# Evacuating and accumulating the expert products on VectorE instead of ScalarE and GpSimd, with another order of the steps in the queue

## The chip, the cores and the metric

The kernel runs on all 8 cores of one Trainium2 chip. Each core computes one of the eight sequences of the batch, with no exchange between them. The time is that of the slowest core, in device microseconds; lower is better. A core has TensorE (PE in the profile; its weight loads are PEld), VectorE (DVE), ScalarE (ACT), GpSimd (POOL) and SyncE (SP), each working through its own list of instructions in order.

## The reference, cut to what matters

```python
# x: (8, 4096, 1024); 16 heads of 64, chunks of 128
q, k = elu(x @ Wq.T + bq) + 1, elu(x @ Wk.T + bk) + 1
v = x @ Wv.T + bv
# per chunk of 128 tokens, state (S, z) carried on:
scores = tril(qi @ ki.T)
num = scores @ vi + qi @ S
den = sum(qi * (cumsum(ki) + z), -1)
out = num / den; S += ki.T @ vi; z += sum(ki)
x = layernorm(x + out @ Wo.T + bo)
# mixture: 8 experts, 1024 x 1024, all computed
gates = softmax(x @ gate_w.T + gate_b)
w = gates where among the two largest, else 0
ffn = sum_e w[:, e] * (x @ expert_w[e].T + expert_b[e])
x = layernorm(x + ffn)
```

## The kernel before

One sequence of 4096 tokens is cut into 8 superchunks (`s`) of 512 tokens, each of 4 chunks (`c`) of 128. The Python program writes one instruction list per engine; an engine takes its list strictly in that order, and `B.wait` puts a semaphore wait into it. So the order in which the program emits work is the order of each engine. A superchunk goes through these stages:

- **Projections** (`proj_core`, L371). Q and K are computed in two waves each of 32 matmuls of 512 columns (L384) into the PSUM buffers `q2`, `q3`; after each wave `emit_phi` evacuates four tiles (two ScalarE activations L407, L412 and one VectorE operation L418 each), and then `ffn_drain(..., limit=2)` (L396) emits up to two steps of the expert queue of the superchunk before. Behind K come the transposes of K (L438) with copies on VectorE (L447), and V (L460, L466) with ScalarE evacuation (L476). Then `ln2_out(s-1)` writes the output of the superchunk before.
- **Scan** (L1029 to L1046). For each chunk: scores (L565), the update of the state S (`sz_part`, L616, L623, L637), the numerator and denominator (`numden_div`, L681, L686), and, one chunk behind, `tail_chunk` (transpose L729, output projection L747 and L753, residual L767, first layer norm) and `tail_b` (cast, transpose L808, gates L825 to L868). Each of these steps hands over from TensorE to VectorE or ScalarE and back. Behind `tail_b(s, c-1)` stands `ffn_drain(s, limit=3)` (L1042).
- **Expert stretch** (L1052 to L1054). `x_stream(s+1)` is emitted first: 8 loads of `xT` pieces on POOL's queue into two landing buffers, each followed by a cast on VectorE (L366). Then `ffn_drain` takes all but `hold = 6` steps of the queue; those six are left for the next projections. In the last superchunk nothing is held.

The expert queue `ffnq` of a superchunk has 36 steps: 4 bias steps (`emit_ffn_bias`, 2 matmuls, L897) and then 32 expert steps (expert outer, chunk inner; `emit_ffn_exp`, 16 matmuls of 512 columns, L924). `ffn_drain` takes steps from the head only, and stops when the head's chunk has not gone through `tail_b` yet. Steps use the PSUM buffers `q0` and `q1` in turn; the scan uses `q0` and `q1` too. A step's product is evacuated by ScalarE into one of two `ffntmp` buffers (L910, L938, the latter with the gate as scale), and GpSimd adds it to `x1f` (`acc_pool`, L884).

The weights: 12 matrices a superchunk (Q, K, V, O, then experts e0 to e7, numbers `m` 0 to 11) pass through three SBUF slots. `free_and_feed(mat)` is called when a matrix has been used for the last time; it emits the load of the next matrix of the sequence into the freed slot, half on SP's queue and half on POOL's. Q and K (`m < 2`) are loaded in 8 pieces of 256 KB, even ones on SP's queue and odd ones on POOL's, each waiting for the piece before it on its queue (L286). In the first superchunk the weights come as f32 in halves through a landing buffer that takes the third slot, are cast by VectorE and ScalarE in turn (L261, L264) and are stored as bf16 for the superchunks behind it.

Of the kernel before, what the change touches and what calls it, by code (L numbers as in the profile page):

```python
# [88 lines left out]
def build():  # L89
# [39 lines left out]
    ffn_tmp = [sb(f"ffntmp{j}", [128, 1024], F32) for j in range(2)]  # L129
# [206 lines left out]
    ffn_tmp_i = [0]  # L336
    ffn_tmp_free = [[], []]
# [33 lines left out]
    def proj_core(s):  # L371
        def proj_qk(mat, dstbf, donearr, bias_col):
            src = wb[wslot[mat]]
            vpe_f = [None] * KB
            for wv in range(2):
# [20 lines left out]
                ffn_drain(s_cur[0], limit=2)  # L396
# [479 lines left out]
    def acc_pool(c, evac_ev):  # L876
        j2 = evac_ev[2]
        B.wait("POOL", evac_ev[0], evac_ev[1])
        if stt_val[c] is None:
            B.wait("POOL", "cdv", x1_apply[c])  # L880
        else:
            B.wait("POOL", "cpl", stt_val[c])
        B.wait("POOL", "dtap", tap_guard[0])
# [5 lines left out]
        return vadd  # L889

    def emit_ffn_bias(c, qi):
# [14 lines left out]
        j2 = ffn_tmp_i[0]  # L906
        ffn_tmp_i[0] ^= 1
        B.wait("ACT", "cpe", vpe)
        B.waits("ACT", ffn_tmp_free[j2])
        vac = B.op("ACT", lambda e, qi=qi, j2=j2: e.activation(  # L910
            ffn_tmp[j2][:], quad[qi][:], AF.Copy), inc="cac")
        qset(qi, (0, 1), [("cac", vac)])
        acc_pool(c, ("cac", vac, j2))
# [227 lines left out]
```

How the kernel before makes its waits and increments, by code:

```python
    def wait(self, eng, cname, val):  # L56
        if val is None or val <= 0:
            return
        w = self.waited[eng]
        if w.get(cname, 0) >= val:
            return
        w[cname] = val
        h = self.ctr[cname][0]
        self.streams[eng].append(lambda e, h=h, v=val: e.wait_ge(h, v))
# [14 lines left out]
        def run(e, fn=fn, h=h, k=k):  # L79
            fn(e).then_inc(h, k)
```

## Time and profile before

| | |
|---|---|
| Time, median of two runs | 2881.48 us (2866.7 and 2896.25) |
| Profiled execution, its own time | 2877.57 us |
| Its span, first to last instruction, slowest core (core 6) | 2875.8 us |
| Busy: PE, PEld | 1881.8 us (65%), 911.1 us (32%) |
| Busy: DVE, ACT, POOL | 700.0 us (24%), 858.0 us (30%), 816.5 us (28%) |
| Granted TensorE clock, mean of a core | 0.785 to 0.791 of full speed |
| Spans of the eight cores | 2850.6 to 2875.8 us |
| HBM | 105 GB/s over the span |

The largest shares of the chain of work that ended last:

```profile
PE 49%; DMA 15%; ACT 12%; DVE 11%; issue 10%; POOL 1%; DVEq 0%; ACTq 0%; SPq 0%; POOLq 0%
```

The profile is of one execution, on its slowest core. Busy time of PE includes overlap between matmuls. In the timeline a row has start, duration, engine, line, operation, output and inputs, count, and in brackets the idle time before it with what ended it; rows of one engine that follow each other closely are merged, and matmul records can be missing by a few in a row. The granted clock is a share of 2.4 GHz: 1.2 GHz would be 0.5.

### The profile page before, as it was taken

The numbers are of one execution on the slowest core, as the hardware profiler recorded it, in microseconds if no ns is written. First come the engines' busy times: TensorE is split into PE (matmuls) and PEld (weight loads), VectorE is DVE, ScalarE is ACT, GpSimd is POOL, SyncE is SP. The second block draws the span as 40 slices with busy tenths as digits, with TensorE's granted clock in tenths as the row PEclk, the third lists the DMA queues.
The fourth block names the chain that finished last, engine by engine and source line by source line (L and its number), as shares of the span: only waits on it lengthen the run. The fifth ranks groups of instructions, "written<-read, shape, count | busy, mean of one in ns | idle before, by whom it ended". The sixth has DMA issues, their size and how long they took to land.

```text
span 2875.8 us, 27448 instructions; the slowest of 8 cores (2850.6 to 2875.8 us)
## 1 busy us (share of the span) xinstructions
PE 1881.8 (65%) x9992; PEld 911.1 (32%) x10144; DVE 700.0 (24%) x1168; ACT 858.0 (30%) x974; POOL 816.5 (28%) x553
## 2 busy tenths in 40 slices
PE   1464455764799449864598547974499646994496
PEld 0132222332344224332244323432244323442243
DVE  1232300143202431043202332034211432024301
ACT  1322223322233223332234222332233222332232
POOL 1000234200462006410273005520174004620065
PEclk8665678875799559975699758995599757995698
DMA  5530366520333213430144103341144202432031
GB/s 176 199 140 15 121 232 231 164 86 15 110 125 123 76 44 131 126 132 14 60 147 147 74 15 125 120 150 37 52 140 135 106 15 103 132 117 81 37 107 69
DMA packets 63354, 303.99 MB, mean 106 GB/s; under 512 B 8172, under 2 KB 8428, under 8 KB 43766
## 3 DMA queue, kind: packets, MB, share of 16 engines
q1 hardware_dynamic: 34326, 163.80, 16.6%
q0 software_dynamic: 28896, 138.43, 14.0%
q8 instruction: 83, 1.36, 0.2%
q14 instruction: 49, 0.40, 0.0%
HBM read 260.26 MB, written 41.94 MB: 105 GB/s over the span
## 4 chain that ended last, share of the span: by engine, by line
PE 49%; DMA 15%; ACT 12%; DVE 11%; issue 10%; POOL 1%; DVEq 0%; ACTq 0%; SPq 0%; POOLq 0%
PE q L924 23%; PE q L747 6%; DMA wb<-escr 6%; DMA wb<-ewT 4%; PE q L460 4%; PE q L384 4%; DMA xtl<-xT 2%; PE q L753 2%; PE q L466 2%; PE q L565 2%; ACT L838 1%; DVE x1f L767 1%; DVE S_f L637 1%; ACT wb L264 1%; DMA out<-osb 1%
## 5 line engine op out<-in xcount | busy, mean ns | idle before, releaser
L884 POOL TENSOR_TENSOR x1f<-ffntmp,x1f 128x1024 f32<-128x1024 f32 x288 | 674.7, 2350 | 1330.1 <-ACT ffntmp L910 996.1
L924 PE MATMUL q<-wb,x1t_bf 128*128 128x512 bf16 x4015 | 914.8, 387 | 74.9 <-ACT ffntmp L938 63.0
L924 PEld LDWEIGHTS q<-wb,x1t_bf 128*128 128x128 bf16 x4096 | 406.4, 100 | 583.1 <-issue 121.8
L938 ACT ACTIVATE ffntmp<-q,w_all 128x1024 f32<-128x1024 f32 x256 | 285.5, 1117 | 552.6 <-PE q L924 483.9
L384 PE MATMUL q<-xt_bf,wb 128*128 128x512 bf16 x1001 | 241.8, 393 | 143.2 <-DMA wb<-escr 56.9
L747 PE MATMUL q<-wb,attnTb 128*128 128x512 bf16 x480 | 179.4, 554 | 54.8 <-ACT attnTb L738 54.8
L418 DVE SCALAR_TENSOR_TENSOR qt_bf<-etmp 128x512 bf16<-128x512 f32 x64 | 44.2, 693 | 630.6 <-ACT etmp L412 630.6
L198 POOL DMA_DIRECT2D wb<-escr x126 | 69.3, 550 | 442.3 <-PE q L466 213.3
L384 PEld LDWEIGHTS q<-xt_bf,wb 128*128 128x128 bf16 x1024 | 100.6, 100 | 279.1 <-issue 173.8
L565 PE MATMUL q<-qt_bf,ktz 128*128 128x128 bf16 x512 | 53.3, 287 | 141.2 <-DVE qtz L543 141.2
L460 PE MATMUL q<-wb,xt_bf 128*128 128x512 bf16 x496 | 123.7, 403 | 15.0 <-DVE ktm_bf L447 13.0
L808 PE MATMUL q<-id_bf,x1c_bf 128*128 128x128 bf16 x256 | 32.7, 307 | 150.3 <-ACT x1c_bf L801 150.3
L767 DVE TENSOR_TENSOR x1f<-q,x0c 128x1024 f32<-128x1024 f32 x32 | 39.2, 1225 | 323.9 <-PE q L753 323.9
L747 PEld LDWEIGHTS q<-wb,attnTb 128*128 128x128 bf16 x512 | 66.5, 134 | 160.2 <-issue 150.6
L781 ACT ACT_TABLE_LOAD x25 | 32.1, 1283 | 282.5 <-DVE mnv L778 282.5
L366 DVE CAST xt_bf<-xtl 128x512 bf16<-128x512 f32 x64 | 91.0, 1438 | 96.6 <-DMA xtl<-xT 96.4
L681 PE MATMUL q<-vext_bf,msc_bf 128*128 128x65 bf16 x512 | 42.5, 206 | 105.0 <-DVE msc_bf L585 92.0
L530 ACT ACTIVATE ktz<-kt_bf,pmask_s 128x1024 bf16<-128x1024 bf16 x64 | 69.9, 1140 | 90.0 <-PE q L565 83.8
L565 PEld LDWEIGHTS q<-qt_bf,ktz 128*128 128x128 bf16 x512 | 46.2, 132 | 149.9 <-issue 149.9
L418 DVE SCALAR_TENSOR_TENSOR kt_bf<-etmp 128x512 bf16<-128x512 f32 x64 | 44.3, 692 | 188.9 <-ACT etmp L412 188.8
L864 PE MATMUL q<-id_bf,w_bfs 128*8 128x128 bf16 x32 | 8.5, 264 | 122.2 <-DVE w_bfs L857 122.2
L407 ACT ACTIVATE etmp<-q,bqc_s 128x512 f32<-128x512 f32 x64 | 44.7, 699 | 144.3 <-PE q L384 135.8
(85 smaller groups left out, 1729.8 us busy)
## 6 DMA issues: line engine op xcount, KB each, us to landing
wb<-escr SPq DMA_DIRECT2D x70, 1024.0 KB, 5.1
wb<-escr POOLq DMA_DIRECT2D x70, 1024.0 KB, 6.2
wb<-ewT SPq DMA_DIRECT2D x16, 2048.0 KB
escr<-wb SPq DMA_DIRECT2D x12, 2048.0 KB, 7.8
xtl<-xT POOLq DMA_DIRECT2D x64, 256.0 KB, 3.3
x0c<-x POOLq DMA_DIRECT2D x32, 512.0 KB, 4.3
out<-osb POOLq DMA_DIRECT2D x32, 512.0 KB, 2.9
wb<-escr SPq DMA_DIRECT2D x56, 256.0 KB, 2.9
```

The costliest lines, as they stand in the source:

```text
L198: return B.op(eng, lambda e, o=out_ap, i=in_ap: e.dma_start(o, i), inc=cname, k=16)
L366: vc = B.op("DVE", lambda e, k=k, j=j: e.tensor_copy(xt_bf[:, k * 512:(k + 1) * 512], xt_land[j][:]), inc="cdv")
L384: fn = lambda e, src=src, k=k, f=f: e.matmul(quad[2 + (f % 4) // 2][:, ((f % 4) % 2) * 512:((f % 4) % 2 + 1) * 512], src[:, k * 1024 + f * ...
L418: e.scalar_tensor_tensor(d[:, f * 512:(f + 1) * 512], et[:], 1.0, et2[:], ALU.min, ALU.add), inc="cdv")
L460: B.op("PE", lambda e, src=src, k=k, c=c, qi=qi, hh=hh: e.matmul(quad[qi][:, hh * 512:(hh + 1) * 512], xt_bf[:, k * 512 + c * 128: k * 512 ...
L530: vkz = B.op("ACT", lambda e, c=c, par=par, mcol=mcol: e.activation(ktz[:].rearrange("p (h w) -> p h w", w=128)[:, par::2, :], kt_bf[:].re ...
L565: fn = lambda e, h=h, f=f, c=c, qi=qi, hh=hh: e.matmul(quad[qi][:, hh * 128:(hh + 1) * 128], ktz[:, h * 128:(h + 1) * 128], qt_bf[:, f * 5 ...
L747: B.op("PE", lambda e, src=src, k=k, hh=hh, j=j: e.matmul(quad[0][:, hh * 512:(hh + 1) * 512], attnT_bfp[j][:, k * 128:(k + 1) * 128], src ...
L767: vres = B.op("DVE", lambda e, j=j, c=c: e.tensor_tensor(x1f[:, c * 1024:(c + 1) * 1024], quad[0][:], x0c[j][:], ALU.add), inc="cdv")
L884: vadd = B.op("POOL", lambda e, c=c, j2=j2: e.tensor_tensor(x1f[:, c * 1024:(c + 1) * 1024], ffn_tmp[j2][:], x1f[:, c * 1024:(c + 1) * 102 ...
L924: fn = lambda e, src=src, k=k, c=c, qi=qi, hh=hh: e.matmul(quad[qi][:, hh * 512:(hh + 1) * 512], x1t_bf[:, c * 1024 + k * 128: c * 1024 + ...
L938: vac = B.op("ACT", lambda e, c=c, qi=qi, e_i=e_i, j2=j2: e.activation(ffn_tmp[j2][:], quad[qi][:], AF.Copy, scale=w_all[:, c * 8 + e_i: c ...
```

## The change

`ffntmp` and `acc_pool` go. A step's product is now taken from PSUM by one VectorE operation, `scalar_tensor_tensor`, that multiplies it by the gate (or by 1.0 in a bias step) and adds it to `x1f` in place; the buffer `q0` or `q1` is free when that is done. The waits that ScalarE and GpSimd had stand on VectorE's list. The queue is filled with the 32 expert steps first and the 4 bias steps behind them. `hold` is 12 instead of 6, and the limit after each projection wave is 3 instead of 2. One more `ffn_drain(s, limit=2)` stands behind `numden_div` in each chunk. A count per expert says when its weights are free; in this order it says so at the same step as before. `ln2_out` waits for VectorE's counter instead of GpSimd's.

```diff
@@ proj_qk
-                ffn_drain(s_cur[0], limit=2)
+                ffn_drain(s_cur[0], limit=3)
@@ acc_pool goes
-        vadd = B.op("POOL", lambda e, c=c, j2=j2: e.tensor_tensor(
-            x1f[:, c * 1024:(c + 1) * 1024], ffn_tmp[j2][:],
-            x1f[:, c * 1024:(c + 1) * 1024], ALU.add), inc="cpl")
-        stt_val[c] = vadd
-        ffn_tmp_free[j2] = [("cpl", vadd)]
+    def acc_wait_dve(c):
         if stt_val[c] is None:
-            B.wait("POOL", "cdv", x1_apply[c])
+            B.wait("DVE", "cdv", x1_apply[c])
         else:
-            B.wait("POOL", "cpl", stt_val[c])
+            B.wait("DVE", "cdv", stt_val[c])
@@ emit_ffn_exp (emit_ffn_bias likewise, with 1.0 for the gate)
-        B.wait("ACT", "cpe", vpe)
-        B.wait("ACT", "cdv", w_done[c])
-        B.waits("ACT", ffn_tmp_free[j2])
-        vac = B.op("ACT", lambda e, c=c, qi=qi, e_i=e_i, j2=j2: e.activation(
-            ffn_tmp[j2][:], quad[qi][:], AF.Copy,
-            scale=w_all[:, c * 8 + e_i: c * 8 + e_i + 1]), inc="cac")
-        qset(qi, (0, 1), [("cac", vac)])
-        vadd = acc_pool(c, ("cac", vac, j2))
+        B.wait("DVE", "cpe", vpe)
+        B.wait("DVE", "cdv", w_done[c])
+        acc_wait_dve(c)
+        B.wait("DVE", "dtap", tap_guard[0])
+        vstt = B.op("DVE", lambda e, c=c, qi=qi, e_i=e_i:
+                    e.scalar_tensor_tensor(
+                        x1f[:, c * 1024:(c + 1) * 1024],
+                        quad[qi][:],
+                        w_all[:, c * 8 + e_i: c * 8 + e_i + 1],
+                        x1f[:, c * 1024:(c + 1) * 1024],
+                        ALU.mult, ALU.add), inc="cdv")
+        stt_val[c] = vstt
+        qset(qi, (0, 1), [("cdv", vstt)])
@@ ffn_drain
+            pick = None
             step = ffnq[0]
             c = step[-1]
-            if c > ffn_done_c[0]:
+            if c <= ffn_done_c[0]:
+                pick = 0
+            if pick is None:
+                if limit is None:
+                    raise RuntimeError("ffn_drain: no ready step on full drain")
                 break
-            ffnq.pop(0)
+            step = ffnq.pop(pick)
...
-                if c == CPS - 1:
+                exp_cnt[e_i] += 1
+                if exp_cnt[e_i] == CPS:
                     free_and_feed(4 + e_i)
@@ the main loop
+            for e_i in range(NE):
+                exp_cnt[e_i] = 0
+                for cc in range(CPS):
+                    ffnq.append(("e", e_i, cc))
             for cc in range(CPS):
                 stt_val[cc] = None
                 ffnq.append(("b", cc))
-            for e_i in range(NE):
-                for cc in range(CPS):
-                    ffnq.append(("e", e_i, cc))
...
                 prev_attn_evs = numden_div(s, c)
+                if stage >= 4:
+                    ffn_drain(s, limit=2)
                 if c < CPS - 1:
                     scores_part(s, c + 1)
...
-            hold = 6 if s + 1 < nsc else 0
+            hold = 12 if s + 1 < nsc else 0
             ffn_drain(s, limit=max(0, len(ffnq) - hold))
```

## Rows read from the trace of the kernel before

**Rows 1.** Windows, superchunk 3: us; busy (count) of PE, PEld, DVE, ACT, POOL; clock; DMA.
```profile
1084.00:1170.00 86.00, 85.05 (x378) 38.14 (x386) 12.09 (x6) 26.63 (x24) 61.42 (x35) 0.97 0.40 141
1170.00:1235.00 65.00, 57.32 (x255) 25.21 (x258) 8.31 (x12) 24.62 (x35) 26.54 (x20) 0.97 0.41 123
...
1266.00:1418.00 152.00, 65.61 (x513) 38.56 (x516) 55.40 (x113) 41.06 (x50) 13.41 (x15) 0.59 0.16 59
```

**Rows 2.** Timeline, a bias step in the scan, and an output projection of superchunk 4.
```profile
988.46 0.26 PE L864 MATMUL q<-id_bf,w_bfs 128*8 128x128 bf16 x1 [3.81 <-DVE w_bfs L857]
989.26 1.01 PE L897 MATMUL q<-ebias,wT_all 8*128 8x512 bf16 x2 [0.53 <-DVE wT_all L868]
...
990.42 1.02 ACT L910 ACTIVATE ffntmp<-q 128x1024 f32<-128x1024 f32 x1 [3.71 <-PE q L897]
...
991.59 1.03 PE L616 MATMUL q<-vext_bf,ktm_bf 128*64 128x64 bf16 x16 [1.32 <-ACT ffntmp L910]
...
997.64 6.18 PE L747 MATMUL q<-wb,attnTb 128*128 128x512 bf16 x15 [1.64 <-ACT attnTb L738]
...
1295.78 5.59 PE L747 MATMUL q<-wb,attnTb 128*128 128x512 bf16 x15 [1.86 <-ACT attnTb L738]
```

**Rows 3.** Timeline, start of the expert stretch of superchunk 3, last two rows superchunk 4.
```profile
1083.12 0.74 DVE L366 CAST xt_bf<-xtl 128x512 bf16<-128x512 f32 x2
...
1084.28 4.02 PE L924 MATMUL q<-wb,x1t_bf 128*128 128x512 bf16 x9
...
1088.52 8.40 PE L924 MATMUL q<-wb,x1t_bf 128*128 128x512 bf16 x38 [0.22 <-issue]
...
1093.57 11.57 POOL L884 TENSOR_TENSOR x1f<-ffntmp,x1f 128x1024 f32<-128x1024 f32 x5
1095.48 10.39 DVE L366 CAST xt_bf<-xtl 128x512 bf16<-128x512 f32 x2 [3.02 <-DMA xtl<-xT]
...
1432.37 8.04 DVE L366 CAST xt_bf<-xtl 128x512 bf16<-128x512 f32 x2 [2.94 <-DMA xtl<-xT]
...
1434.24 4.85 PE L924 MATMUL q<-wb,x1t_bf 128*128 128x512 bf16 x11 [3.06 <-ACT ffntmp L938]
```

**Rows 4.** Timeline, end of that expert stretch and the projections behind it.
```profile
1170.11 1.11 ACT L938 ACTIVATE ffntmp<-q,w_all 128x1024 f32<-128x1024 f32 x1 [2.34 <-PE q L924]
1171.43 2.34 POOL L884 TENSOR_TENSOR x1f<-ffntmp,x1f 128x1024 f32<-128x1024 f32 x1 [1.11 <-ACT ffntmp L938]
...
1173.71 0.57 POOL L198 DMA_DIRECT2D wb<-escr  x1
...
1188.15 1.02 PE L384 MATMUL q<-xt_bf,wb 128*128 128x512 bf16 x4 [1.84 <-DMA wb<-escr]
...
1195.92 7.07 PE L384 MATMUL q<-xt_bf,wb 128*128 128x512 bf16 x31
...
1199.84 0.55 POOL L198 DMA_DIRECT2D wb<-escr  x1
...
1218.43 1.86 PE L384 MATMUL q<-xt_bf,wb 128*128 128x512 bf16 x4 [2.49 <-DMA wb<-escr]
...
1227.80 7.07 PE L384 MATMUL q<-xt_bf,wb 128*128 128x512 bf16 x31
```

**Rows 5.** Timeline, from the last K tile to V.
```profile
1240.60 4.61 DVE L447 CAST ktm_bf<-q 128x1024 bf16<-128x1024 f32 x4
...
1243.11 4.63 PE L460 MATMUL q<-wb,xt_bf 128*128 128x512 bf16 x15 [0.22 <-issue]
```

**Rows 6.** Lines of the whole span: the VectorE group nearest to the new operation.
```profile
L767 DVE TENSOR_TENSOR x1f<-q,x0c 128x1024 f32<-128x1024 f32 x32 | 39.2, 1225 | 323.9 <-PE q L753 323.9
```

**Rows 7.** Timeline, end of the program.
```profile
2852.51 1.11 ACT L938 ACTIVATE ffntmp<-q,w_all 128x1024 f32<-128x1024 f32 x1 [2.34 <-PE q L924]
...
2862.93 0.69 DVE L973 BATCH_NORM_STATS2 lnst<-x1f 128x6 f32<-128x512 f32 x1
```

**Rows 8.** Waits of the whole span, a row of the first superchunk's weight staging.
```profile
DVE wb L261 <- DMA wb<-ewT: 161.9, 6, 36.8
```

More of the change, by code:

```diff
@@ L128, in build @@
     x1f = sb("x1f", [128, 4096], F32)
-    ffn_tmp = [sb(f"ffntmp{j}", [128, 1024], F32) for j in range(2)]
     x1c_bf = sb("x1c_bf", [128, 1024], BF16)
@@ L335, in build @@
     stt_val = [None] * CPS
-    ffn_tmp_i = [0]
-    ffn_tmp_free = [[], []]
     stt_guard = [0] * CPS
@@ L905, in emit_ffn_bias @@
                 vpe = B.op("PE", fn, inc="cpe")
-        j2 = ffn_tmp_i[0]
-        ffn_tmp_i[0] ^= 1
-        B.wait("ACT", "cpe", vpe)
-        B.waits("ACT", ffn_tmp_free[j2])
-        vac = B.op("ACT", lambda e, qi=qi, j2=j2: e.activation(
-            ffn_tmp[j2][:], quad[qi][:], AF.Copy), inc="cac")
-        qset(qi, (0, 1), [("cac", vac)])
-        acc_pool(c, ("cac", vac, j2))
+        B.wait("DVE", "cpe", vpe)
+        acc_wait_dve(c)
+        B.wait("DVE", "dtap", tap_guard[0])
+        vstt = B.op("DVE", lambda e, c=c, qi=qi: e.scalar_tensor_tensor(
+            x1f[:, c * 1024:(c + 1) * 1024], quad[qi][:], 1.0,
+            x1f[:, c * 1024:(c + 1) * 1024], ALU.mult, ALU.add), inc="cdv")
+        stt_val[c] = vstt
+        qset(qi, (0, 1), [("cdv", vstt)])
     def emit_ffn_exp(s, e_i, c, qi):
@@ L932, in emit_ffn_exp @@
                     B.op("PE", fn)
-        j2 = ffn_tmp_i[0]
-        ffn_tmp_i[0] ^= 1
-        B.wait("ACT", "cpe", vpe)
-        B.wait("ACT", "cdv", w_done[c])
-        B.waits("ACT", ffn_tmp_free[j2])
-        vac = B.op("ACT", lambda e, c=c, qi=qi, e_i=e_i, j2=j2: e.activation(
-            ffn_tmp[j2][:], quad[qi][:], AF.Copy,
-            scale=w_all[:, c * 8 + e_i: c * 8 + e_i + 1]), inc="cac")
-        qset(qi, (0, 1), [("cac", vac)])
-        vadd = acc_pool(c, ("cac", vac, j2))
+        B.wait("DVE", "cpe", vpe)
+        B.wait("DVE", "cdv", w_done[c])
+        acc_wait_dve(c)
+        B.wait("DVE", "dtap", tap_guard[0])
+        vstt = B.op("DVE", lambda e, c=c, qi=qi, e_i=e_i:
[5 more added lines that the diff above has]
+                        ALU.mult, ALU.add), inc="cdv")
+        stt_val[c] = vstt
+        qset(qi, (0, 1), [("cdv", vstt)])
         if s == 0 and c == 0 and e_i == NE - 1:
-            emit_tap("ffn", x1f[:, 0:1024], [("cpl", vadd)])
+            emit_tap("ffn", x1f[:, 0:1024], [("cdv", vstt)])
     ffn_qi = [0]
     s_cur = [0]
+    ffnq_owner = [0]
+    exp_cnt = [0] * NE
     def ffn_drain(s, limit=None):
         n = 0
+        so = ffnq_owner[0]
         while ffnq and (limit is None or n < limit):
+            pick = None
             step = ffnq[0]
             c = step[-1]
-            if c > ffn_done_c[0]:
+            if c <= ffn_done_c[0]:
[3 more added lines that the diff above has]
+                    raise RuntimeError("ffn_drain: no ready step on full drain")
                 break
-            ffnq.pop(0)
+            step = ffnq.pop(pick)
+            c = step[-1]
             qi = ffn_qi[0]
@@ L962, in ffn_drain @@
                 _, e_i, c = step
-                emit_ffn_exp(s, e_i, c, qi)
-                if c == CPS - 1:
+                emit_ffn_exp(so, e_i, c, qi)
+                exp_cnt[e_i] += 1
+                if exp_cnt[e_i] == CPS:
                     free_and_feed(4 + e_i)
@@ L971, in ln2_out @@
             j = c % 2
-            B.wait("DVE", "cpl", stt_val[c])
+            B.wait("DVE", "cdv", stt_val[c])
             B.op("DVE", lambda e, c=c: e.bn_stats(
@@ L1022, in build @@
             ffn_done_c[0] = -1
+            ffnq_owner[0] = s
+            for e_i in range(NE):
+                exp_cnt[e_i] = 0
+                for cc in range(CPS):
+                    ffnq.append(("e", e_i, cc))
             for cc in range(CPS):
```

5 lines of the change are left out of this document (removed).

## The prediction

> **What bounds the kernel now.** I read the page first: TensorE is busy for 65% of the span, the other engines for 30% or less, so nothing is full all the time. The windows by stage come next [rows 1], because a mean over stages hides which wait ends last in each. In the expert stretch TensorE is busy for 85 of 86 us at 0.97 of its clock: there its own matmuls are the bound, and evacuating and adding are hidden. In the projections with the held steps it is busy for 57 of 65 us. In the scan it is busy for 66 of 152 us at 0.59: a chain of short steps that hands over between engines, most of it at 1.2 GHz. The timeline then gives the waits at the seams, and the reader should look at four places: the bias step in the scan [rows 2], the start of the expert stretch [rows 3], the weight loads before Q and K [rows 4], and the copies before V [rows 5].
>
> So ScalarE and GpSimd, which the change relieves, bound nothing in the expert stretch. What counts is where the steps go and who waits for whom at the seams.
>
> **What the change does to the order.** The queue gives only its head. Behind `tail_b(c-1)` chunk c-1 is ready and c is not. Before, one bias step went out there; now one expert step does (e0 of chunk c-1), three a superchunk. The new drain behind `numden_div` finds at the head a step of a chunk that is not ready, so it emits nothing. The expert stretch then has 33 - 12 = 21 steps (before 33 - 6 = 27, one of them a bias step). The projections take 12 held steps in 3+3+3+3 (e6, e7, four bias steps) instead of 6 in 2+2+2.
>
> **Scan.** Before: the bias matmuls start at 989.26, ScalarE evacuates in 1.02 us, and the state's matmuls start at 991.59, as they share the buffer: 2.33 us [rows 2]. TensorE takes its list in order, so an expert step there hides behind nothing: the whole of it lies in the chain. Its 16 matmuls have the shape and count of an output projection, which also starts from idle and takes 5.6 to 6.2 us (the rows record 15 of 16) [rows 2]; I take 5.6. The new evacuation isn't in the trace. The nearest row is L767, a two-input VectorE operation of the same size from PSUM, 1.225 us [rows 6]. At least it costs that; GpSimd's 2.34 us for the same sum [rows 4] is the upper bound. I take 1.25, so the gap of 1.3 us becomes 1.55. That makes 5.6 + 1.55 = 7.15 instead of 2.33: +4.8 us. The clock is then up for the next matmuls (L616, L623, in 2.0 us now), and I give 0.8 back. +4.0 us at 24 places is **+96**. Bounds for one place: +1.5 (below, clock) and +6.0 (no give-back, slower evacuation), so +36 to +144.
>
> A rule of the Trainium skill bears on the give-back (TensorE: Matmul & The Clock Gate, section "Loop structure matters more than you think"): a copy out of PSUM between two groups of matmuls doesn't bring the clock down. By that the projection behind the step would run fast as well. No stretch of rows 2 shows this, since no long step stands there; it is rival B.
>
> **Start of the expert stretch.** Here the saving falls due: three expert steps (3.45 us each, the distance of two evacuations in the stretch) and a bias step (1.0) are gone, -11.4 us. But `x_stream` stands ahead on VectorE's list: 8 casts, paced by their loads two by two, from 1083.12, the last pair landing at 1095.48 [rows 3]. ScalarE wasn't behind them; the new operation is. TensorE runs two steps (9 matmuls at 1.2 GHz in 4.02 us, the rest at 2.4 GHz [rows 3], 9.1 us in all, to 1092.2) and then waits until the casts (1096.3) and one evacuation (1097.6) are done: 5.4 us. It restarts slowly: 11 matmuls took 4.85 us after a gap of 3.06 us in superchunk 4, where 11 at full clock take 2.4 [rows 3]. I put 2.1 on it (what those 9 above lose against full clock). The net is -3.9 here. In superchunk 4, whose last pair lands at 1432.37, 3 us later in its stretch, the new gap would be 8.3; but the stretch of before already has 3.06 of gap and 2.4 of slow restart [rows 3]: -11.4 + 8.3 + 2.1 - 5.5 = -6.5. I take -5 for six superchunks: **-30** (between -18 and -48). In the last one no `x_stream` is emitted: **-11.4**. In the first the stretch is bound by the staging of the weights (VectorE alone waits 161.9 us for it [rows 8]), and steps taken out save **0**; down to -5.
>
> One more thing is in that working: the last two casts took 10.39 us beside five GpSimd additions, and 0.74 for a pair without them [rows 3]. The additions are gone, so I count the short ones. If they stayed long, each stretch would lose 9.5 us more. The Trainium skill says why they were long (SBUF — State Buffer, section "Who interferes with whom"): VectorE and GpSimd hold one pair of ports in turn, for a whole instruction.
>
> **Loads before Q and K.** Let T0 be the end of e5's last step, 1169.9, which frees the slot for the next Q. GpSimd's half of the pieces starts only at 1173.71, because its list has that step's addition first [rows 4]. Four pairs then take 14.4 us and the last Q matmuls of the first wave end at 1189.17, T0 + 19.3. The two held steps e6 c0, c1 lay inside that wait, for free. Now: no addition ahead, the load starts at T0 and the wave ends at T0 + 15.5; nothing lies inside the wait. Then e6 c0 to c2 (10.4), the second Q wave (6.9) and e6 c3 (3.5): K's load can start at T0 + 36.3. Before, it was ordered at 1195.9 (T0 + 26.0), started on GpSimd's queue at 1199.84 (T0 + 29.9), and ended the wait at 1218.43, 18.6 us behind. Then the first K wave ends 1.9 later. With 18.6 now: T0 + 54.9, wave's end T0 + 56.8, two expert steps from a slow clock 7.8, a bias step 0.5, second K wave 7: T0 + 72.1. Before it ended at 1234.8, T0 + 64.9 [rows 4]. **+7.2**. What is late next is V. Behind the last wave three bias steps go out; two need VectorE behind the four tiles of `emit_phi`, and three evacuations of 1.25 stand ahead of the K copies (start 1240.60, V at 1243.11 [rows 5]). The first copy ends at 1245.8 instead of 1241.8 and V follows: +2.7. So +9.9 a seam, seven seams, and 2 more in the first, where GpSimd had no addition ahead: **+71**. Bounds: a wait 3 us shorter or longer, and the bias steps for nothing or twice: +6 to +14 a seam, +42 to +98.
>
> **End.** Before, the last layer norm started while e7 still ran; its last statistics start at 2862.93, 10.5 us behind the last product (2852.4) [rows 7]. Now it is emitted behind four bias steps: four evacuations one after another (6.4 us), then three chunks of norm at 3.15 and 1.6 for the table: 17.4. **+7** (+4 to +10).
>
> **Hidden elsewhere.** In the stretch an evacuation of 1.25 to 2.34 us fits twice into the two buffers' 6.9 us: 0. ScalarE's and GpSimd's freed time: 0, as neither ends a wait there, apart from the start of the loads, counted above.
>
> **Sum.** 96 - 30 - 11.4 + 0 + 71 + 7 = +133 us. Against the profiled execution's own 2877.6 us that is 3010 us; the median of the runs shown is 2881.5, 0.1% above it, so I leave it.
>
> **The rivals.**
> - A, the forecast: slower by the expert steps in the scan and the seams, about 3010.
> - B, the clock stays up behind an expert step through the output projection: L616 and L623 save 0.7, L729 0.5, L747 2.1, so +1.5 a place, +36 instead of +96: 2950. Pushed further, it is the rival of the other side: if the expert step itself ran fast too (3.45 for 5.6), a place would cost -0.65, a place is 4.65 below the forecast, the sum would be +21, 2899, and the kernel would not be slower. It decides from a place price of about 0.9 us on (below that, the sum is under 58 us, and the time within 2%). For it: waves with gaps of 1.8 us stay fast [rows 4]. Against it: in the scan TensorE is idle more than half of the time, the clock is 0.59 [rows 1], and the first matmuls after a gap of 2.5 us were slow again [rows 4].
> - C, the loads before Q and K get much faster without GpSimd's additions. With half the 14.4 us a seam would gain about 14 us more, and the sum is +35: 2912. Against it: the pieces wait for each other, and nothing of the additions lies between them.
> - D, the evacuation costs GpSimd's 2.34 us: 1.1 x 24 in the scan, 3 a seam: 3057. Against it: L767.
>
> **How the numbers follow.** A 0.70, B 0.13 (0.04 of it at its far end), C 0.04, D 0.08; 0.05 for what I don't see, half of it a gain. Range: from B's near end to just over D, 2940 to 3060, which leaves out B's far end, C and half of the unseen. A measurement tells 2%, 58 us, from no change here: faster 0.03, same 0.09, slower 0.88.
>
> **What would show it.** In the profile after: GpSimd nearly without busy time; one L924 group of 16 in the scan behind each gate chain, 5.6 us, and a VectorE operation of about 1.25 us behind it; a gap of 5 us or more after two steps in each expert stretch, ended by VectorE; Q waiting for its load with no expert step inside; K's load starting about 36 us behind T0. The scan would be some 12 us longer a superchunk. It would be wrong if the L747 groups behind an expert step take under 4 us, or if loads take under 10 us.

## The result and the profile after

The changed kernel takes 3040.5 us (median of 11 runs) against 2875.4 (10 runs of the kernel before). The ratio is 1.057, with a 95% interval of 1.054 to 1.060, so it is 5.7% slower: some 165 us by the medians. The medians take in every execution, while ratios, intervals and profiles are of those in which neither half of the chip ran at a lower clock than the other; "one profile" in a table means that only one such was left. The profiled execution spans 3035.0 us on its slowest core, 159.2 more than before.

From the page after: busy times, the chain's shares by engine, and the two groups of the expert steps.

```profile
PE 1935.7 (64%) x10144; PEld 902.1 (30%) x10144; DVE 996.5 (33%) x1456; ACT 542.8 (18%) x686; POOL 142.6 (5%) x265
...
PE 51%; DMA 17%; DVE 13%; ACT 10%; issue 8%; DVEq 1%; POOL 0%; ACTq 0%; SPq 0%; POOLq 0%
...
L912 PE MATMUL q<-wb,x1t_bf 128*128 128x512 bf16 x4096 | 989.7, 407 | 127.6 <-DVE x1f L926 114.6
...
L926 DVE SCALAR_TENSOR_TENSOR x1f<-q,w_all,x1f 128x1024 f32<-128x1024 f32 x256 | 327.6, 1283 | 560.3 <-PE q L912 560.1
```

The relief came as meant: ScalarE is down by 315 us of work and GpSimd by 674. That was not what bound the expert stretch: there TensorE had waited for ScalarE in three stretches of six, 0.9 to 3.1 us each. The new operation takes 1.283 us, and TensorE now waits 114.6 us in the whole span for it.

The windows of the third superchunk's stretch, of its seam (from the end of the stretch to V), and of the next scan (columns as in [rows 1]) show where the time is:

```profile
1131.00:1219.00 88.00, 76.37 (x332) 33.52 (x333) 29.00 (x29) 0.00 (x0) 5.85 (x11) 0.89 0.38 138
1219.00:1307.00 88.00, 68.81 (x304) 29.25 (x302) 29.71 (x33) 21.13 (x34) 5.88 (x11) 0.90 0.34 106
1329.00:1486.00 157.00, 72.15 (x555) 40.19 (x553) 58.26 (x113) 37.89 (x47) 6.36 (x12) 0.67 0.16 57
```

The stretch that was TensorE's alone (85 of 86 us busy [rows 1]) now has 12 us without it, the seam 19.

For all runs I cut a superchunk at five marks of the timeline: **B**, the last copy of the gates (the line L868 of before), where the expert stretch begins; **Q** and **K**, ScalarE's first evacuation of the first Q and K wave; **V**, the first matmul of V; and the last evacuation of V, where the scan begins. Means of superchunks 2 to 7 (scans 2 to 8), us:

| profile | scan | B to Q | Q to K | K to V | V to scan | superchunk | span |
|---|---|---|---|---|---|---|---|
| before | 149.8 | 107.0 | 28.9 | 22.8 | 22.8 | 331.1 | 2875.8 |
| after | 159.4 | 103.0 | 41.2 | 28.1 | 22.4 | 353.8 | 3035.0 |

In before the record of V's first matmul is missing; by its weight load V starts some 0.4 us earlier there, so K to V is 22.4 and the difference to after 5.7 us (it is the same in e8 and e10 below).

### The profile page after: what moved, and what is told of

It reads as the page before. It is cut to its first block, busy times and chain, and to the rows that moved or that the text cites. A ratio compares the mean times of both kernels' runs of the same rounds, so it can differ in the third digit from the quotient of the medians.

```text
span 3035.0 us, 26553 instructions; the slowest of 8 cores (3019.6 to 3035.0 us)
## 1 busy us (share of the span) xinstructions
PE 1935.7 (64%) x10144; PEld 902.1 (30%) x10144; DVE 996.5 (33%) x1456; ACT 542.8 (18%) x686; POOL 142.6 (5%) x265
## 4 chain that ended last, share of the span: by engine, by line
PE 51%; DMA 17%; DVE 13%; ACT 10%; issue 8%; DVEq 1%; POOL 0%; ACTq 0%; SPq 0%; POOLq 0%
PE q L912 26%; DMA wb<-escr 7%; PE q L744 6%; PE q L381 4%; DMA wb<-ewT 4%; PE q L457 4%; DMA xtl<-xT 4%; PE q L750 2%; PE q L463 2%; PE q L562 1%; ACT L835 1%; DVE x1f L926 1%; DVE x1f L764 1%; DVE S_f L634 1%; ACT wb L263 1%
## 5 line engine op out<-in xcount | busy, mean ns | idle before, releaser
L912 PE MATMUL q<-wb,x1t_bf 128*128 128x512 bf16 x4096 | 989.7, 407 | 127.6 <-DVE x1f L926 114.6
L912 PEld LDWEIGHTS q<-wb,x1t_bf 128*128 128x128 bf16 x4096 | 420.8, 104 | 684.7 <-issue 265.3
L926 DVE SCALAR_TENSOR_TENSOR x1f<-q,w_all,x1f 128x1024 f32<-128x1024 f32 x256 | 327.6, 1283 | 560.3 <-PE q L912 560.1
L381 PE MATMUL q<-xt_bf,wb 128*128 128x512 bf16 x1024 | 262.3, 411 | 206.1 <-DMA wb<-escr 119.8
L744 PE MATMUL q<-wb,attnTb 128*128 128x512 bf16 x512 | 173.3, 513 | 44.7 <-ACT attnTb L735 44.7
L805 PE MATMUL q<-id_bf,x1c_bf 128*128 128x128 bf16 x256 | 32.8, 308 | 150.2 <-ACT x1c_bf L798 150.2
L562 PEld LDWEIGHTS q<-qt_bf,ktz 128*128 128x128 bf16 x512 | 46.2, 132 | 149.8 <-issue 149.8
L582 DVE TENSOR_TENSOR msc_bf<-q,maskT_f 128x1024 bf16<-128x1024 f32 x64 | 75.3, 1218 | 30.4 <-PE q L562 30.4
L404 ACT ACTIVATE etmp<-q,bkc_s 128x512 f32<-128x512 f32 x64 | 44.8, 699 | 221.8 <-PE q L381 221.8
L260 DVE CAST wb<-wb 128x4096 bf16<-128x4096 f32 x12 | 27.5, 2292 | 171.3 <-DMA wb<-ewT 98.2
```

What stands on the lines that cost most here:

```text
L381: fn = lambda e, src=src, k=k, f=f: e.matmul(quad[2 + (f % 4) // 2][:, ((f % 4) % 2) * 512:((f % 4) % 2 + 1) * 512], src[:, k * 1024 + f * ...
L404: va = B.op("ACT", lambda e, qi=qi, hh=hh, et=et, bc=bc: e.activation(et[:], quad[qi][:, hh * 512:(hh + 1) * 512], AF.Exp, bias=bc), inc=" ...
L562: fn = lambda e, h=h, f=f, c=c, qi=qi, hh=hh: e.matmul(quad[qi][:, hh * 128:(hh + 1) * 128], ktz[:, h * 128:(h + 1) * 128], qt_bf[:, f * 5 ...
L582: vm = B.op("DVE", lambda e, half=half, qi=qi: e.tensor_tensor(msc_bf[:, half * 1024:(half + 1) * 1024].rearrange("p (h w) -> p h w", w=12 ...
L744: B.op("PE", lambda e, src=src, k=k, hh=hh, j=j: e.matmul(quad[0][:, hh * 512:(hh + 1) * 512], attnT_bfp[j][:, k * 128:(k + 1) * 128], src ...
L912: fn = lambda e, src=src, k=k, c=c, qi=qi, hh=hh: e.matmul(quad[qi][:, hh * 512:(hh + 1) * 512], x1t_bf[:, c * 1024 + k * 128: c * 1024 + ...
```

## The change taken apart

Three kernels make one part of the change each; a fourth makes all of it but the move to VectorE.

**e1, VectorE alone.** After, with the order and the held steps of before:

```diff
-ffn_drain(s_cur[0], limit=3)          +ffn_drain(s_cur[0], limit=2)
-hold = 12 if s + 1 < nsc else 0       +hold = 6 if s + 1 < nsc else 0
-(experts queued first, bias last)     +(bias queued first, experts behind)
```

> One part alone: the products go through VectorE, but the queue has the bias steps first, 6 steps are held and 2 go out behind a wave, as before the change. Theory (the terms of the forecast, by the trace of after): at the start of each expert stretch TensorE has room for one bias and one expert step and then waits for the casts of x, some 8 us and a slow restart of 2, where before it waited 0 to 5.5; at each seam GpSimd's half of the Q and K pieces starts 3.8 us earlier, so 7.6 are saved. Sum near 0, -30 to +40 us. The new wait should be under 9 us, because e0 is not finished while x is loaded, so no weight load falls into it. Rival 1: VectorE's evacuation is itself what costs (a longer chain in the scan, or VectorE too busy): then this part alone takes most of the +160 us. Rival 2: the wait of 11.6 us seen in after comes with VectorE's evacuation whatever the order: then the same wait stands here too.

**e2, order alone.** Before, with the two loops that fill `ffnq` exchanged.

> One part alone: expert steps first and bias steps last in the queue, ScalarE and GpSimd evacuate as before, 6 steps held (two of e7 and the four bias steps), 2 behind a wave. Theory: the scan gets 9 to 10 us longer a superchunk, as in after (+77 in eight), the expert stretch loses three expert steps and one bias step (-11.4 in seven, -80), and at the seam the loads for Q and K are ordered before the projections start, so the load waits go, but the held steps are too short to cover the evacuation waits: about 0. Sum -30 to +20 us. Rival: expert steps in the scan hide in its idle time, then the scan is as long as before and the sum is near -80 us.

**e3, held steps alone.** Before, with

```diff
-ffn_drain(s_cur[0], limit=2)          +ffn_drain(s_cur[0], limit=3)
-hold = 6 if s + 1 < nsc else 0        +hold = 8 if s + 1 < nsc else 0
```

> One part alone: 8 expert steps (all of e6 and e7) held over the projections instead of 6, 3 behind a wave instead of 2; order and evacuation as before. It isolates what it costs that e6 and e7 both lie behind the first Q wave, so that K's weights are ordered later. Theory: K's load is ordered two expert steps and one wave (13.8 us) later and nothing lies in the wait for Q: the end of the K waves comes about 14 us later a seam, +97 us in all (+70 to +110). Rival: K's load is hidden either way, then the sum is within 20 us of before.

With the bias steps first, 12 held steps would be e5, e6 and e7, and the first Q wave would need a slot that e5 frees behind it; so 8, all of e6 and e7, is what answers to after.

**e4, all but VectorE.** After's order, held steps and limit, with the evacuation of before.

> After with the evacuation of before (ScalarE, then GpSimd's addition); queue order, 12 held steps and 3 behind a wave as in after. Theory: scan +77, expert stretches -80 and -5 in the last, seams +14 each and 2 to 3 for the bias steps, +115, together +90 to +125 us; so after's remaining 40 to 70 us are the wait for VectorE behind the casts of x, less the earlier pieces. Rival: all of after's loss is order and held steps, then this takes +150 us or more.

| profile | scan | B to Q | Q to K | K to V | superchunk | span | ratio to before |
|---|---|---|---|---|---|---|---|
| before | 149.8 | 107.0 | 28.9 | 22.8 | 331.1 | 2875.8 | |
| e1 VectorE | 149.4 | 113.6 | 27.7 | 22.2 | 335.7 | 2914.1 | one profile, +38 us |
| e2 order | 158.6 | 113.4 | 29.7 | 21.9 | 345.9 | 2979.3 | one profile, +104 us |
| e3 held steps | 150.3 | 107.2 | 43.4 | 22.5 | 346.0 | 2986.2 | 1.039 (1.034 to 1.044) |
| e4 order, held steps | 159.3 | 96.9 | 43.1 | 27.3 | 349.4 | 3010.8 | 1.049 (1.043 to 1.054) |
| after | 159.4 | 103.0 | 41.2 | 28.1 | 353.8 | 3035.0 | 1.057 (1.054 to 1.060) |

e3 does what was expected of it (+97 expected, +110 measured, the upper end of its range), and nearly all of it stands in one column: Q to K, +14.5 us. Holding e6 and e7 over the first Q wave orders K's weights 14 us later: in superchunk 3 SyncE orders their first piece 21.4 us behind Q, and 7.6 us in before. e4 came out at +135 us, 10 above its range, and its Q to K shows the same 14.2. e1 is at the upper end of its range, with TensorE's wait for the casts at 8.0 to 9.7 us in the six stretches (8 expected). The VectorE part is small: +4.6 us a superchunk alone, +4.4 on top of the rest. So of the 159 us the order and the held steps together make 135, and VectorE makes 24, where e4's expectation had left 40 to 70. The order and the held steps don't add up (104 and 110 alone, 135 together): a good part of e2's loss is a wait of its own, and e4 doesn't have it.

e2 missed its range by over 80 us, and two things were wrong in the expectation. I booked the expert stretch as shorter, but with the bias steps last the six held steps are two experts and four bias steps, so the stretch has 27 expert steps, where it had 26 and a bias step. And it has a wait that I hadn't thought of. Timeline of e2, TensorE and GpSimd, behind e6 of the third superchunk:

```profile
1201.90 0.57 POOL L198 DMA_DIRECT2D wb<-escr  x1
...
1212.88 0.54 POOL L198 DMA_DIRECT2D wb<-escr  x1 [2.99 <-DMA wb<-escr]
1213.43 6.93 POOL L884 TENSOR_TENSOR x1f<-ffntmp,x1f 128x1024 f32<-128x1024 f32 x3
1217.35 3.15 PE L924 MATMUL q<-wb,x1t_bf 128*128 128x512 bf16 x7 [5.40 <-ACT ffntmp L938]
```

Q's pieces wait for each other on GpSimd's list (four between 1201.9 and 1212.9), and the additions stand behind them. With both `ffntmp` full, ScalarE stops, both PSUM buffers fill, and TensorE waits 5.4 us (5.4 to 6.8 in the six). Before, only two steps lay in that time and the buffers took them. This is what moving the additions off GpSimd's list saves if Q's load is ordered early: in e11 and e12 below, with evacuation on VectorE, TensorE has no wait at this place.

## The wait at the start of the stretch

Timeline of after, TensorE, VectorE and GpSimd, third superchunk [answers to rows 3]:

```profile
1131.26 9.11 PE L912 MATMUL q<-wb,x1t_bf 128*128 128x512 bf16 x30
...
1137.19 1.16 POOL L197 DMA_DIRECT2D xtl<-xT  x2 [3.52 <-DVE xt_bf L363]
...
1144.42 0.43 DVE L363 CAST xt_bf<-xtl 128x512 bf16<-128x512 f32 x1 [7.16 <-DMA xtl<-xT]
...
1150.61 0.43 DVE L363 CAST xt_bf<-xtl 128x512 bf16<-128x512 f32 x1 [1.83 <-DMA xtl<-xT]
1150.95 2.47 DVE L926 SCALAR_TENSOR_TENSOR x1f<-q,w_all,x1f 128x1024 f32<-128x1024 f32 x2
1152.38 7.92 PE L912 MATMUL q<-wb,x1t_bf 128*128 128x512 bf16 x26 [11.57 <-DVE x1f L926]
```

TensorE does two steps and waits 11.57 us (9.4 to 11.6 in six stretches, mean 10.5). The forecast had 5.4 us for this superchunk and 8.3 for the fourth, which has 10.1. The mechanism is the forecast's: the evacuations stand behind the casts. But the third pair of x pieces took over 7 us to land, where the other pairs took 3 to 4, here and before. DMA issues of after between 1131 and 1151 us (count, KB each, median us to landing):

```profile
xtl<-xT POOLq DMA_DIRECT2D x6, 256.0 KB, 3.6
wb<-escr SPq DMA_DIRECT2D x1, 1024.0 KB, 8.5
wb<-escr POOLq DMA_DIRECT2D x1, 1024.0 KB, 7.1
```

The load on GpSimd's queue is ordered at 1147.8 us, behind the last x piece. The one on SyncE's, 1 MB too, lies among the x loads (at 1137.4). It goes into e0's slot: three of e0's four steps were done in the scan, the fourth is the first of the stretch, and it frees the slot in the middle of the x loads. Before, e0 ended behind them.

**e5** holds that load back.

```diff
 def free_and_feed(mat):
+    if mat == 4:
+        B.wait("SP", "cdv", xt_cast[KB - 1])
```

> After with one wait more: SyncE orders its half of the weights that follow e0 in its slot only once the last cast of x is done. e0's last step now runs at the start of the expert stretch, so this 1 MB load starts while x is being loaded. Theory: that collision is why TensorE waited 11.6 us there and not the forecast 5.4; without it the x loads take 3 to 4 us each again, the wait falls to 5 to 7 us and the kernel gains 4 to 6 us in each of six or seven stretches, -25 to -40 us against after. The weights are needed eight steps later, so the delay itself costs nothing. Rival: the x loads are slow for another reason (VectorE's or GpSimd's queue), then the wait stays at 10 us or more and the time within 10 us of after.

Timeline of e5, VectorE and TensorE, the same place in the third superchunk:

```profile
1171.68 0.43 DVE L365 CAST xt_bf<-xtl 128x512 bf16<-128x512 f32 x1 [1.40 <-DMA xtl<-xT]
...
1173.45 6.78 PE L914 MATMUL q<-wb,x1t_bf 128*128 128x512 bf16 x17 [6.53 <-DVE x1f L928]
```

The wait falls to 6.5 to 8.6 us (mean 7.4 for 10.5), and the last cast starts 14.9 us behind B, not 17.9. So 3.1 us of the wait are the collision, and B to Q is 2.8 us shorter (100.2). What is left is near the forecast: 6.5 us for 5.4 in superchunk 3, 8.6 for 8.3 in superchunk 4. The casts of e1, where e0 ends later too, are done about as early as those of e5 (14.1 us behind B). The kernel didn't get faster by it, and the expected 25 to 40 us are missed: its superchunks are 3.2 us shorter, but the first one takes 33 us more (3047.5 us of span, one execution). In its expert stretch the weights are staged, and an expert takes 31 to 32 us there, 27 to 28 in after (by SyncE's stores). The added wait stands on SyncE's list, which also loads and stores those weights; that it is the cause is argued, not tested.

**e6** puts an expert step ahead of each x load with its cast.

```diff
 for k in range(KB):
+    if between is not None:
+        between()            # ffn_drain(s, limit=1)
```

> After with the loads and casts of x emitted one by one between the first eight expert steps instead of all ahead of them. VectorE's list then has an evacuation between two casts. Theory: the whole wait (11.6 us and a slow restart of 2) comes from the evacuations standing behind all eight casts; it goes, and the kernel gains 11 to 14 us in each of six stretches, -65 to -85 us against after. Rival: the products' evacuation on VectorE is too slow for the stretch or the casts still hold it up, then the gain is under half of that.

The gain wasn't there: ratio 1.059 (1.053 to 1.064), B to Q 101.9. The one wait had become two, 3.2 to 3.5 and 3.2 to 4.2 us, each with a restart at 1.2 GHz. I took this for more collisions; what it is was seen only in e11. The trace of e6 has the form already: in superchunk 3 GpSimd orders half of a weight matrix at 1137.40 and two x pieces right behind it at 1137.91, and the cast comes at 1145.23.

## The place in the scan

**e7** was meant to be after without steps in the scan.

```diff
 ffn_done_c[0] = c - 1
 if stage >= 4:
-    ffn_drain(s, limit=3)
+    ffn_drain(s, limit=0)
```

> After without steps in the scan: the three expert steps that go out there are left for the expert stretch. Theory: the scan gets 9 to 10 us shorter a superchunk (back to about 150), the stretch gets three steps longer (+10.4) but e0 is no longer finished while x is loaded, so the collision goes (-4 to -6): -3 to -6 a superchunk, -20 to -50 us in all against after. Rival: the steps in the scan do hide part of the expert work, then the kernel gets slower than after.

It took 2914 us, 1.015 (1.012 to 1.018) of before, and 126 us less than after by the medians, far outside the range. The scan is 140.5 us long. The premise was wrong: with the head no longer taken behind `tail_b`, the new drain behind `numden_div`, which emits nothing in after, finds e0 of chunk 0 and chunk 1 ready and sends them out there. Timeline of e7, TensorE and VectorE, at a chunk without such a step (first row) and one with it:

```profile
987.57 1.87 PE L562 MATMUL q<-qt_bf,ktz 128*128 128x128 bf16 x16 [6.35 <-DVE qtz L540]
...
1015.55 3.61 PE L912 MATMUL q<-wb,x1t_bf 128*128 128x512 bf16 x16 [0.68 <-DVE x1f L764]
...
1021.48 0.87 DVE L540 TENSOR_SCALAR qtz<-qt_bf,pmask_s 128x1024 bf16<-128x1024 bf16 x2
...
1022.50 1.05 PE L562 MATMUL q<-qt_bf,ktz 128*128 128x128 bf16 x16 [3.34 <-DVE qtz L540]
```

Behind the numerator TensorE waits 6 to 8 us for VectorE to make the next masked Q (L540). An expert step started there runs at 2.4 GHz: the granted clock rose from 0.50 to 1.00 while the output projection ran (it is 0.97 from 1010.0 to 1015.5) and is still 1.00. The step takes 3.6 us and is over 3.3 us before anyone needs TensorE. The second step of a scan goes out in the last chunk, where no masked Q is left to make; what it fills is the wait for ScalarE's copy ahead of the transposes of `tail_b` (L805), 6.3 us in after and 2.8 in e7. Even the scores behind it are quicker, 1.05 us for 1.87. The same step behind `tail_b` in after (timeline, TensorE and VectorE, answering [rows 2]):

```profile
1029.71 0.27 PE L861 MATMUL q<-id_bf,w_bfs 128*8 128x128 bf16 x1 [3.81 <-DVE w_bfs L854]
...
1030.72 5.16 PE L912 MATMUL q<-wb,x1t_bf 128*128 128x512 bf16 x16 [0.74 <-DVE wT_all L865]
1036.00 1.28 DVE L926 SCALAR_TENSOR_TENSOR x1f<-q,w_all,x1f 128x1024 f32<-128x1024 f32 x1 [5.63 <-PE q L912]
1037.43 0.67 PE L613 MATMUL q<-vext_bf,ktm_bf 128*64 128x64 bf16 x16 [1.55 <-DVE x1f L926]
...
1042.22 6.23 PE L744 MATMUL q<-wb,attnTb 128*128 128x512 bf16 x16 [1.46 <-ACT attnTb L735]
```

Here nothing covers it: it starts from idle (granted clock 0.50 until 1033), and the state's matmuls wait for its evacuation.

**e9** has neither drain, **e10** is the kernel before with its drain moved to the other place.

```diff
 prev_attn_evs = numden_div(s, c)
+if stage >= 4:                        (e10 only)
+    ffn_drain(s, limit=2)
...
-        ffn_drain(s, limit=3)
+        ffn_drain(s, limit=0)
```

> After with neither of the two drains in the scan. In the run without the drain behind tail_b the other one, behind numden_div, had steps to send out (e0 of chunks 0 and 1), and the scan was 140 us long; so that run did not measure a scan without steps, and this one does. Theory: the two steps behind numden_div hide in TensorE's wait for the masked Q (6 to 7 us), so without them the scan stays at 140 us and the expert stretch gets two steps, 6.9 us, longer: +50 us in eight superchunks against that run, about 2960. Rival: those steps cost something in the scan, then the scan gets shorter than 140 us and the time stays near 2914.

> The kernel before with one thing moved: the drain of the scan stands behind numden_div instead of behind tail_b. Queue, evacuation and held steps as before; two bias steps go out there instead of three behind tail_b. Theory: the place decides. A step behind tail_b lies in the chain, behind numden_div it hides: the scan falls from 150 to about 140 us a superchunk, the stretch gets one bias step (1 to 2 us) more: -55 to -75 us, 2.0 to 2.6% faster than before. Rival: it is the kind of step or VectorE's evacuation that made the scan short, then it is within 20 us of before.

| profile | steps in the scan | scan | B to Q | superchunk | span |
|---|---|---|---|---|---|
| before | 3 bias, behind `tail_b` | 149.8 | 107.0 | 331.1 | 2875.8 |
| after | 3 expert, behind `tail_b` | 159.4 | 103.0 | 353.8 | 3035.0 |
| e9 | none | 141.3 | 110.1 | 343.9 | 2963.8 |
| e7 | 2 expert, behind `numden_div` | 140.5 | 106.2 | 339.0 | 2912.5 |
| e10 | 2 bias, behind `numden_div` | 142.3 | 110.9 | 326.6 | 2843.0 |

e9's time came as expected (ratio 1.031, 1.028 to 1.034), and so did its scan. Its other parts didn't: B to Q is only 3.9 us longer than in e7 and not 6.9, because the wait at the start of the stretch is shorter (mean 6.9 us for 9.4), and the first superchunk is 20 us longer, so part of the agreement is luck. It gives the prices in the scan: behind `tail_b` a bias step costs (149.8 - 141.3) / 3 = 2.8 us and an expert step (159.4 - 141.3) / 3 = 6.0 us; behind `numden_div` two expert steps cost nothing. The kernel before paid for its place too: e10, one profile, is 33 us shorter. That is half of what was expected. The scan gave its 7.5 us, but the stretch lost 3.9: TensorE waits 1.6 to 4.9 us there (mean 2.7) for a `ffntmp`, in all six stretches, where before it did so in three (0.9 to 3.1). A second bias step at the head fills the `ffntmp` buffers while the additions stand behind the x loads; that reading is argued, not tested.

## Versions from the findings

**e8**: VectorE's evacuation, bias steps first, e6's x order, and only e7 held, one step behind each wave.

```diff
-ffn_drain(s_cur[0], limit=3)          +ffn_drain(s_cur[0], limit=1)
-hold = 12 if s + 1 < nsc else 0       +hold = 4 if s + 1 < nsc else 0
```

> A version from the findings: evacuation on VectorE as in after, bias steps first in the queue as before, x loads and casts between the first eight steps, only the four steps of e7 held, one behind each wave. Theory: no wait for casts in the stretch; Q's load has e6 (13.8 us) to cover its 15, K's load is ordered before the first Q wave. The first K wave's evacuations come some 10 us earlier a seam than before: -60 to -90 us against the kernel before (2790 to 2815). Rival: the seams' waits only change their place (one step of 3.45 us does not cover the 4.7 us of evacuating a wave, the casts slip into the first Q wave), then it is within 30 us of before.

**e11**: the drain behind `numden_div` alone, two steps ahead of each x load with its cast, and

```diff
+for e_i in range(NE):
+    for cc in range(CPS):
+        ffnq.append(("e", e_i, cc))
+        if e_i == NE - 1:
+            ffnq.append(("b", cc))
-ffn_drain(s_cur[0], limit=3)          +ffn_drain(s_cur[0], limit=2)
-hold = 12 if s + 1 < nsc else 0       +hold = 8 if s + 1 < nsc else 0
```

> A version from all findings. From after: evacuation on VectorE, experts first. The scan's only drain stands behind numden_div. Each load and cast of x follows two expert steps. Held over the projections are the four steps of e7 with a bias step behind each, two steps (one expert, one bias) behind a wave, so that the loads of Q and K are ordered before. Theory: scan 140 us, no wait for casts, Q's load covered but for 2 us, waves as in the hold-4 run: 305 to 312 us a superchunk for 331, -170 to -200 us against before, 0.93 to 0.94 of its time. Rival: the gains overlap (loads collide again in the stretch, bias evacuations hold up the waves), then 0.95 to 0.97.

Both were right at the seam and wrong in the stretch: their spans are 27 and 35 us under before's, where 60 to 90 and 170 to 200 were expected. e8: 0.993 (0.988 to 0.997), Q to K 22.9, B to Q 111.9, with one wait of 3.3 to 5.6 us a stretch. e11: 0.988 (0.986 to 0.990), scan 141.0, Q to K 22.9, but B to Q 121.1, with four waits a stretch. Timeline of e11, GpSimd, VectorE and TensorE, one of them:

```profile
1066.48 0.53 POOL L197 DMA_DIRECT2D wb<-escr  x1 [24.00 <-PE q L914]
1067.00 1.07 POOL L197 DMA_DIRECT2D xtl<-xT  x2
1075.26 0.43 DVE L365 CAST xt_bf<-xtl 128x512 bf16<-128x512 f32 x1 [7.94 <-DMA xtl<-xT]
...
1077.03 3.57 PE L914 MATMUL q<-wb,x1t_bf 128*128 128x512 bf16 x8 [4.19 <-DVE x1f L928]
```

GpSimd's list has the next weight load, which waits for the expert's end, ahead of the x loads. The x loads so start with the weight load, land 8 us later, and VectorE's list has the cast ahead of the evacuations. A load in a list that also has long waits has to be written well ahead of its use. **e12** does that: piece k+2 is ordered right behind the cast of piece k, four expert steps earlier and so ahead of the weight wait that it stood behind.

```diff
+x_load(0); x_load(1)
 for k in range(KB):
     between()
-    x_load(k)
     (cast of piece k)
+    if k + 2 < KB:
+        x_load(k + 2)
```

> The e11 version with one thing moved: the load of an x piece is put on GpSimd's list right behind the cast two pieces earlier, not just ahead of its own cast. In e11's trace each expert's end has a wait of 3.1 to 4.3 us for VectorE and a restart at 1.2 GHz, four a stretch: the x loads stand on GpSimd's list behind the weight load that waits for the expert's end, land 7 to 8 us later beside that 1 MB, and the evacuations wait behind the cast. Theory: with the loads ahead these four waits and restarts go, 14 us and some 6 to 8 us: the time from the stretch's start to the first Q wave's end falls from 120 to about 101 us, some 18 us in each of six stretches, -100 to -120 us, about 2730, 0.95 of before. Rival: the weight loads collide with x wherever it is put and the gain is under 40 us.

Timeline of e12, GpSimd, third superchunk:

```profile
1047.77 0.54 POOL L197 DMA_DIRECT2D wb<-escr  x1 [23.00 <-PE q L923]
1049.50 0.54 POOL L197 DMA_DIRECT2D xtl<-xT  x1 [1.20 <-DVE xt_bf L372]
1057.01 0.54 POOL L197 DMA_DIRECT2D xtl<-xT  x1 [6.97 <-DVE xt_bf L372]
1062.48 0.54 POOL L197 DMA_DIRECT2D wb<-escr  x1 [4.93 <-PE q L923]
```

The piece ordered at 1049.50 is cast at 1063.31. It still lands slowly beside the weight load (7.7 us; the one ordered at 1057.01 takes 3.7), and nobody waits for it. So it is the place in the list that took the waits away, and the rival of the expectation, that the loads collide wherever x is put, is right on the loads and wrong on the time.

The windows of e12, third superchunk: stretch with the first Q wave, seam, scan.

```profile
1037.00:1137.00 100.00, 99.47 (x446) 44.36 (x446) 36.31 (x35) 0.00 (x0) 8.96 (x17) 0.96 0.45 149
1137.00:1204.00 67.00, 62.74 (x285) 27.73 (x282) 27.47 (x33) 24.22 (x37) 2.86 (x6) 0.97 0.33 117
1205.00:1344.00 139.00, 66.09 (x532) 38.33 (x529) 56.72 (x112) 37.68 (x47) 6.38 (x12) 0.67 0.18 65
```

| profile | scan | B to Q | Q to K | K to V | superchunk | span | ratio to before |
|---|---|---|---|---|---|---|---|
| e8 | 149.6 | 111.9 | 22.9 | 20.8 | 327.2 | 2849.1 | 0.993 (0.988 to 0.997) |
| e11 | 141.0 | 121.1 | 22.9 | 22.1 | 329.4 | 2840.9 | 0.988 (0.986 to 0.990) |
| e12 | 140.0 | 100.0 | 22.9 | 22.2 | 307.2 | 2710.8 | 0.943 (0.941 to 0.945) |

e12 takes 2711 us, 5.7% less than before and 10.8% less than after (2711.4 / 3040.5). B to Q fell by 21 us from e11, TensorE is busy for 99.5 of 100 us there and has no wait over 0.6 us in any of the six stretches, and all six superchunks agree within 0.6 us. The one move that takes the waits away is the test of what caused them; e6's two waits have the same form, but weren't tried by themselves.

## Why the prediction was right, point by point

The forecast was 3010 us, range 2940 to 3060, slower; measured 3040. Its sum was +133 us, the profile shows +159. The mechanism is the forecast's: expert steps in the scan's chain, K's weights ordered late, evacuations behind the casts. The sum is closer than its terms, and that part is luck. Over the six whole superchunks the scans are 14 us below their forecast, the start of the stretch 29 above it and Q to V 23 above; the first superchunk, its scan and the end are together 9 below.

- **Scan, +4.0 us a place forecast.** The scans got 9.6 us longer (9.9 in the first), 3.2 a place. The expert step took 5.16 us in the row above, its evacuation 1.28 (1.25 taken), and the gap 1.55 as worked out. Two sizes were off: the step (5.6 taken), and the give-back: from L613 to the projection it is 4.8 us, 6.05 before [rows 2], 1.25 less and not 0.8. Together they are the 0.8 us a place.
- **Rival B, the clock stays up.** It doesn't. L613 behind the evacuation is at 2.4 GHz (0.67 us for 1.03), and so is the transpose behind it, but the projection takes 6.23 us. The granted clock is 1.00 up to 1040.1 and 0.50 from 1042.2 on; two more hand-overs with little work between them lie in there. The Trainium skill's rule (TensorE: Matmul & The Clock Gate, "Loop structure matters more than you think") is stated for matmuls that follow the copy immediately, and for the copy itself the trace agrees: the matmuls behind its gap of 1.55 us are fast. Drawing it out to the projection, as rival B did, went beyond it.
- **Rivals C and D.** The loads didn't get faster: from GpSimd's first piece of Q's weights to Q it is 14.8 us in after and 14.9 before (superchunk 3). The evacuation costs 1.28 us, not 2.34.
- **Start of the stretch, -5 and 3.8 less for the earlier pieces forecast, -4.0 measured in B to Q.** This is the term that was most mis-sized, by 4.8 us a stretch. The wait is 11.6 us for 5.4 in superchunk 3 and 10.1 for 8.3 in superchunk 4; e5 gives 3.1 us of it to the collision. I had counted who stands behind the casts, and not that the freed slot of e0 starts its own load in the middle of them. The change moves e0's end, and the load moves with it.
- **The casts become short without GpSimd's additions.** They did: 0.43 us each, where two took 10.39 [rows 3]. So far the trace agrees with the Trainium skill (SBUF — State Buffer, "Who interferes with whom"). But one of those two casts took 9.95 us by itself, beside four additions in a row of 2.3 us each, which is more than one turn of a whole instruction; no run here shows why.
- **Loads before Q and K, and V behind them, +13.7 us from Q to V forecast, +17.6 measured.** The late order of K's weights is as forecast; e3 isolates it at 14.5 us. The rows of after, answering [rows 4, 5] (timeline, TensorE and GpSimd):

```profile
1246.52 7.07 PE L381 MATMUL q<-xt_bf,wb 128*128 128x512 bf16 x32
...
1257.64 0.54 POOL L197 DMA_DIRECT2D wb<-escr  x1 [25.00 <-PE q L912]
...
1277.37 1.86 PE L381 MATMUL q<-xt_bf,wb 128*128 128x512 bf16 x4 [4.13 <-DMA wb<-escr]
...
1301.95 1.01 PE L885 MATMUL q<-ebias,wT_all 8*128 8x512 bf16 x2 [5.35 <-DVE x1f L897]
...
1306.99 3.62 PE L457 MATMUL q<-wb,xt_bf 128*128 128x512 bf16 x16
```

  K's load starts at 1257.6 on GpSimd's list and its wait ends at 1277.4, 19.7 us behind it (18.6 taken). The third bias step waits 5.35 us for VectorE. Most of the miss lies in what I took for before: the seam I read (54.4 us from Q to V) was the longest of six, their mean is 51.7, as K's load wait there was 2.49 us, the longest too. One superchunk more in the timeline would have shown it.
- **First superchunk.** +18 us from its B to the next B, the scan behind it included; forecast 24.
- **End.** -11.4 + 7 forecast, -5.6 measured (132.1 us behind the last B for 137.8). The four evacuations took 4.61 us together (6.4 taken).
- **What was read off the program.** That the drain behind `numden_div` emits nothing is right. I took it as a dead line and didn't ask what it would have done alive: e7, where it works and the other doesn't, is 122 us shorter in span. TensorE is idle there, and the profile shows it (the 7.6 us before L565 in superchunk 3 and others like it, 141.2 us in the whole span for "DVE qtz L543"). Another such place has no drain in any of these kernels: the wait for ScalarE's copy before the last transposes of a scan (L808), 7.7 us in before and still 7.4 in e12, where e0 of the third chunk is ready. That a step would hide there is not tested.

## What to carry to other kernels

A step used as filler is worth what the idle time at its exact place in the engine's list is worth: the same 16 matmuls make the scan 6.0 us longer behind one hand-over and no longer behind another. When work moves, follow what its end releases: here the slot's next load moved into other loads, and a held expert put off K's weights by 14 us. And in a list shared by DMA issues and work, a load has to stand ahead of every wait that isn't its own; ordering each x load four expert steps earlier, ahead of one weight wait more, was worth 4.6% (spans of 2840.9 and 2710.8 us, e11 and e12).

## What the runs showed that I had not expected

- An expert step costs 3.6 us if it starts right behind the output projection and 4.9 to 5.3 where TensorE has been idle: the place decides the clock as well as the cover.
- A queue of chained pieces on GpSimd's list stops its additions for 11 us, and through two buffers and ScalarE that stops TensorE for 5.4 (e2).
- An x piece of 256 KB lands in about 3 us alone and takes 7 to 8 beside a weight load of 1 MB.
